# One AdaLN transformer block: the order of its first loads and scalings, and the queue of its expert rows

## What is computed

```python
mod = (_silu(c) @ wmod).reshape(8, 6, 1, 256)
sa, ca, ga, sb, cb, gb = (mod[:, i] for i in range(6))   # ga, gb: magnitude at least 0.25
h = _layernorm(x) * (1 + ca) + sa
x = x + ga * attention(h)      # W_pack to 16 q and 8 k, 8 v heads of 128; rope; 2-tap conv; window 128; W_o
h = _layernorm(x) * (1 + cb) + sb
x = x + gb * experts(h)        # h + top 4 of 32 experts (176 wide, 128 slots each) + shared expert (704 wide)
```

## Time and profile before

| | us |
|---|---|
| median of 3 runs | 781.05 |
| lowest, highest | 780.67, 781.09 |
| profiled execution, its time | 779.91 |
| its span, first to last instruction | 778.1 |
| TensorE busy in it | 744.3 (96%) |
| VectorE, ScalarE, GpSimd busy | 536.7, 441.9, 425.7 |
| DMA, mean over the span | 109 GB/s |

### The profile page before, as it was taken

The page is one execution under the profiler, slowest core; times in us unless marked ns, Lnnn a source line. Parts: engine busy times, 40 slices in busy tenths (PEclk is TensorE's granted clock), DMA queues, the critical chain, the costliest instruction groups (busy, mean ns, idle before and its releaser), DMA issues.

```text
span 778.1 us, 12285 instructions
## 1 busy us (share of the span) xinstructions
PE 744.3 (96%) x3858; PEld 617.3 (79%) x3858; DVE 536.7 (69%) x1676; ACT 441.9 (57%) x1145; POOL 425.7 (55%) x337
## 2 busy tenths in 40 slices
PE   3899999999999999999999999999989999989998
PEld 3688778888888888788888888888876777756765
DVE  4698777679877777987786798778664234534283
ACT  4687766766876576677657667766553222212110
POOL 0644445554556378646637865654544527656366
PEclk9999999999999999999999999999999999999999
DMA  8950006700005011100401101050358669997762
GB/s 301 313 130 1 2 1 207 249 1 1 1 1 174 17 39 47 39 0 1 141 23 39 46 28 45 31 161 2 122 148 265 147 189 288 271 253 149 183 203 81
DMA packets 62351, 84.45 MB, mean 109 GB/s; under 512 B 6312, under 2 KB 50229, under 8 KB 62288
## 3 DMA queue, kind: packets, MB, share of 16 engines
q1 hardware_dynamic: 52880, 73.52, 31.1%
q0 software_dynamic: 7680, 8.95, 5.8%
q10 hardware_dynamic: 1728, 1.21, 0.6%
HBM read 54.88 MB, written 33.51 MB: 114 GB/s over the span
## 4 chain that ended last, share of the span: by engine, by line
PE 78%; DVE 10%; DMA 5%; ACT 3%; issue 2%; SPq 1%; POOL 1%; ACTq 0%; POOLq 0%
PE PJ L1292 23%; PE OUT L1396 12%; PE U L1385 6%; PE U L1345 6%; PE U L1374 5%; DMA xe<-slot_rows 4%; PE U L1546 3%; PE U L1344 3%; PE U L1386 3%; PE OUT L1492 3%; PE U L1492 3%; PE U L1292 2%; PE XB L1292 2%; PE XB L1368 1%; DVE U L945 1%
## 5 line engine op out<-in xcount | busy, mean ns | idle before, releaser
L736 POOL TENSOR_TENSOR qsw<-qsw,sinT 128x512 f32<-128x512 f32 x96 | 124.2, 1294 | 214.8 <-ACT qsw L523 214.1
L536 ACT ACTIVATE U<-U,nmax 128x128 f32<-128x128 f32 (+1 forms) x256 | 98.9, 386 | 79.2 <-DVE nmax L945 79.0
L945 DVE CUSTOM_DVE_ANT_0 U<-U,mask 128x128 f32<-128x128 f32 (+1 forms) x256 | 86.6, 379 | 74.9 <-PE U L1345 74.7
L1396 PE MATMUL OUT<-wo,oT 128*128 128x256 f32 x512 | 131.5, 380 | 0.0
L1292 PE MATMUL PJ<-hT_hi,w_hi 128*128 128x512 f32 x256 | 113.5, 443 | 4.3 <-DVE hT_lo L919 3.9
L1292 PE MATMUL PJ<-hT_lo,w_hi 128*128 128x512 f32 x256 | 102.2, 399 | 0.0
L1292 PE MATMUL PJ<-hT_hi,w_lo 128*128 128x512 f32 x256 | 102.2, 399 | 0.0
L955 DVE TENSOR_SCALAR prob<-U,rinv 128x128 f32<-128x128 f32 (+1 forms) x256 | 95.1, 413 | 4.5
L522 ACT ACTIVATE qsw<-PJ 64x512 f32<-64x512 f32 x96 | 57.0, 593 | 67.1 <-PE PJ L1292 61.7
L740 POOL TENSOR_TENSOR qr<-qr,qsw 128x512 f32<-128x512 f32 x64 | 82.9, 1295 | 18.5 <-DVE qr L933 14.8
L1396 PEld LDWEIGHTS OUT<-wo,oT 128*128 128x128 f32 x512 | 87.6, 191 | 6.6
(11 more groups left out here) (201 smaller groups left out, 1557.3 us busy)
## 6 DMA issues: line engine op xcount, KB each, us to landing
wgu<-in_dram SPq DMA_DIRECT2D x32, 352.0 KB
expert_sum<-blank SPq DMA_DIRECT2D x3, 2176.0 KB, 17.7
wd<-in_dram SPq DMA_DIRECT2D x16, 352.0 KB
slot_rows<-blank SPq DMA_DIRECT2D x1, 4624.0 KB, 26.8
xe<-slot_rows SPq DMA_DIRECT2D x16, 289.0 KB
late_sums<-expert_sum SPq DMA_DIRECT2D x9, 512.0 KB, 9.8
wraw<-in_dram SPq DMA_DIRECT2D x8, 512.0 KB, 12.1
bcm<-mod_rows SPq DMA_DIRECT2D x8, 512.0 KB, 6.7
```

The costliest lines, as they stand in the source:

```text
L536: last = act.activation(U[n % 3][:, a:z], U[n % 3][:, a:z], ACT.Exp, scale=-1.0, bias=nmax[:, n % 4, j:j + 1], accum_out=rsum[:, n % 4, j: ...
L736: pool.tensor_tensor(pair3(qsw[:, n % NQSW, :]), pair3(qsw[:, n % NQSW, :]), both(sinT[:, :]), ALU.mult).then_inc(t2_done, 1)
L945: last = dve.tensor_tensor_reduce(out=U[n % 3][:, a:z], in0=U[n % 3][:, a:z], in1=mask[:, a:z], scale=-float(HD) ** -0.5, scalar=3.4e38, o ...
L1396: last = pe.matmul(OUT[b][:, t * H:(t + 1) * H], oT[:, n % NOT, t * PN:(t + 1) * PN], wo[:, head, :], start=(head == 0 and t == 0), stop=( ...
```

## The change

The first third of wmod becomes the first transfer of ScalarE's queue, ahead of the rope tables; on SyncE's queue `xin` changes places with `ident`. The second half of the first pair's features is scaled by VectorE (`prepare_second_half`) instead of ScalarE; ScalarE's two rounded copies then wait for both halves, and only one chunk of W_pack is split before the features instead of two. The first projection waits for one low part, and for the other ahead of its fourth matmul. After the transposes of `xin` TensorE does ten transposes of `ident` into the bank XB, whose result is not used. In the expert stage the rows of experts 8 to 31 are issued by ScalarE at the end of each odd slot, with the two waits that SyncE had.

```diff
+        WARM = 10
...
             sp.dma_start(c_sb[:, :], c_in).then_inc(ld_c, 16)
+            sp.dma_start(xin[:, :, :], x_pair(0)).then_inc(ld_xin, 16)
             sp.dma_start(ident[:, :], ident_t).then_inc(ld_ident, 16)
-            sp.dma_start(xin[:, :, :], x_pair(0)).then_inc(ld_xin, 16)
-            wm_src = wmod.rearrange("(c p) n -> p c n", p=PN)
-            sp.dma_start(wm[:, :, 0:2 * H], wm_src[:, :, 0:2 * H]).then_inc(ld_wm, 16)
...
             for e in range(RING, E, 2):
                 i = (e // 2) % HALF
-                sp.wait_ge(xe_ps, e + 2 - RING)
-                sp.wait_ge(told, (e - RING) // 2 + 1)
-                slot_rows(e, i)
                 sp.wait_ge(gu_ps, e + 2 - RING)
                 gate_up_weights(e, i)
...
             own = Chain(act, act_own)
+            act.dma_start(wm[:, :, 0:2 * H], wm_src[:, :, 0:2 * H]).then_inc(ld_wm, 16)
             act.dma_start(cosT[:, :], cos_t).then_inc(ld_const, 16)
...
             def prepare_hi(p, c):
-                act.wait_ge(ht_used, HC * p + (c + 1))
+                act.wait_ge(ht_used, HC * p + (c + 1) if p > 0 else HC)
...
             prepare_norm(0)
-            for n in range(W_FIRST - 1):
+            w_high(0)
+            act.wait_ge(modt_done, 1)
+            prepare_h(0, 0, U[0])
+            prepare_hi(0, 0)
+            prepare_hi(0, 1)
+            for n in range(1, W_FIRST):
                 w_high(n)
-            act.wait_ge(modt_done, 1)
-            for c in range(HC):
-                prepare_h(0, c, U[c])
-                prepare_hi(0, c)
-            w_high(W_FIRST - 1)
...
+                if n % 2 == 1 and n - 1 + RING < E:
+                    e = n - 1 + RING
+                    i = (e // 2) % HALF
+                    act.wait_ge(xe_ps, e + 2 - RING)
+                    act.wait_ge(told, (e - RING) // 2 + 1)
+                    act.dma_start(xe[:, 2 * i:2 * i + 2, :], slots_d.rearrange("(s e) h -> s e h", e=E)[:, e:e + 2, :]).then_inc(ld_xe[i], 16)
...
+            def prepare_second_half():
+                dve.wait_ge(modt_done, 1)
+                dve.wait_ge(ht_ps, 2)
+                for b in range(2):
+                    last = dve.tensor_scalar(hst[:, 1, b * S:(b + 1) * S], U[1][:, b * S:(b + 1) * S], modT[:, 3, b:b + 1],
+                                             modT[:, 1, b:b + 1], ALU.mult, ALU.add)
+                last.then_inc(ht_used, 1)
...
             mod_features()
-            for n in range(W_FIRST - 1):
-                w_low(n)
+            w_low(0)
+            prepare_second_half()
             for c in range(HC):
                 prepare_lo(0, c)
-            w_low(W_FIRST - 1)
+            for n in range(1, W_FIRST):
+                w_low(n)
...
                 for n, (c, a, b_) in enumerate(steps):
+                    if n == 3 and second is not None:
+                        pe.wait_ge(h_lo_done, second)
...
                 if l == 0:
-                    pe.wait_ge(h_lo_done, HC * (p + 1))
+                    pe.wait_ge(h_lo_done, HC * p + 1)
...
             for c in range(HC):
                 prepare_t(0, c, U[c])
+
+            for n in range(WARM):
+                pe.transpose(XB[:, 0:PN], ident[:, :], ident[:, :])
```

More of the change, by code:

```diff
@@ L290, in w_chunks @@
             return W_ORDER.index(head_of(l) * HD // WC) + 1
+        wm_src = wmod.rearrange("(c p) n -> p c n", p=PN)
         def x_pair(p):
@@ L1286, in _, with halves @@
         def _(pe):
-            def halves(out_ap, pieces, hi_lo):
+            def halves(out_ap, pieces, hi_lo, second=None):
                 (w1, w2), (x1, x2) = hi_lo
@@ L1330, in project @@
                        ((lambda c: w_hi[j][:, c, cols], lambda c: w_lo[j][:, c, cols]),
-                        (lambda c: hT_hi[:, p % 2, c, :], lambda c: hT_lo[:, p % 2, c, :]))).then_inc(pj_ps, 1)
+                        (lambda c: hT_hi[:, p % 2, c, :], lambda c: hT_lo[:, p % 2, c, :])),
+                       second=HC * (p + 1) if l == 0 else None).then_inc(pj_ps, 1)
             def scores(n):
```

## The result

The change makes the kernel faster by 0.8%: the ratio to the kernel before is 0.992, with an interval of 0.9899 to 0.9941, so 4.6 to 7.9 us of 781. The medians are 776.21 (20 runs) and 782.73; applied to the 781.05 of the prediction the ratio gives 774.8, just under the range. A second series gave 0.9904 (0.9867 to 0.9942). Ratios are of fast runs alone: a run over 1.5% above the fastest of its kernel is left out of them, though not of the medians. The forecast of 778.65, a gain of 2.4 us, had the sign and the places right and about 40% of the size; 776.21 lies near the lower end of the range.

A forecast was written before the change was run, and what follows sets the result against it. It took the start to be bound by a chain, continuous TensorE work between, and the experts by transfers. Setup -1.2 and experts -1.2 made -2.4, on the median of 781.05 giving 778.65; range 775.0 to 781.5, holding 8 in 10.

The forecast's parts named there:

- Weights first: Setup: the modulation matmuls start at 6.8, between 6.2 and 8.4, and everything behind them moves 1.6 us.
- Two engines: Setup: VectorE's scaling takes 0.86 us and ScalarE's second half leaves the line; first projection about 14.9, 3.3 us earlier.
- Identity transposes: Setup, TensorE: ten cost 2.5 us in a gap of 2.3; a faster clock in the first projection saves 0.7 of 1.55.
- The wait that takes its place: VectorE, before the second xin's statistics: stands over 3 us until that transfer lands, taken as 31.2 (31.1 to 31.6).
- The setup's term: Setup: earlier statistics of the second xin plus 0.5 us of shorter w_lo, a gain of 1.2 us (0.3 to 1.5).
- ScalarE's issues: Experts: ScalarE idles 1.90 us before the next silu, so an issue of slot rows below that costs nothing.
- The slower rival: Experts: ScalarE gets stuck in its issues of slot rows ahead of silus, losing 3.1 us; 782.95, chance 0.12.
- The experts: Expert stage: slot rows issued earlier fill idle DMA time, a gain of 1.2 us (0 to 1.8).
- the bytes stay: Expert stage: weights, rows and scatter-adds fill the DMA engines, so only idle DMA time, 1.8 us, can be gained.
- the rival in which the weights keep up: Experts: queue order, not bytes, was the limit; most of 6.1 us idling goes, 4.5 counted; 775.35, chance 0.21.
- The room at GpSimd's end: End: GpSimd's last sum ends 6.0 us before the span's end, leaving room for the 1.2, or a rival's 4.5.
- The clock in the new wait: Setup: TensorE idles during VectorE's wait, its clock halves, the next projection takes 1.55 us more; 779.85, chance 0.12.

The follow-up runs named there:

- one_engine: The changed kernel with ScalarE scaling both halves of the first pair's features, as before; ratio 0.9958 to the kernel before.
- rows_late: The kernel before with slot rows on ScalarE's queue, each load but the first issued two slots later than in the change; ratio 0.9936 to the kernel before.
- setup_only: The changed kernel with the twelve loads of slot rows back on SyncE's queue, the setup alone; ratio 0.9942 to the kernel before.
- fewer_adds: The changed kernel without the scatter-adds of the last three experts (29 to 31); ratio 0.9943 to the kernel before.
- wm_on_sp: The changed kernel with the modulation weights back on SyncE's queue, third behind ident and xin; ratio 1.0023 to the kernel before.
- rows_only: The kernel before with the twelve loads of slot rows on ScalarE's queue, that part alone; ratio 0.9932 to the kernel before.
- both: The changed kernel with the second xin ahead of the rest of wmod and GpSimd's last sum on VectorE; median 773.22, ratio 0.9917 to the kernel before.

## Why the prediction was right, and where its terms were off

*What bounds, and where.* Right: the gains sit in the first two slices and the experts, and between them nothing moves (from 38.01 to 627.29 is 589.28 us, before 40.30 to 629.45 589.15).

*Weights first.* The modulation product started at 7.52, not 6.8: its transposes waited for ident until 6.90, and ident stands behind xin now. Inside the bounds of 6.2 to 8.4.

*Two engines.* Off. VectorE's pair took 0.99 us (0.86 taken, bounds 0.69 to 1.02), but the step priced it as a gain, and one_engine shows none: both copies now wait for both halves, and VectorE's half ends 0.2 us before ScalarE would have ended it. First projection at 15.97, forecast 14.9.

*Identity transposes.* Their size was right (2.30 us against 2.5), and what they buy was taken at 0.7 of a possible 1.55; it is 1.23 at ScalarE. Their worth at the end, none, follows from the wait.

*The wait that takes its place.* Right in kind and in the row that shows it: VectorE idle before the statistics, ended by the second xin. Its size was 1.79 instead of over 3, since the landing bound was wrong: 31.1 to 31.6 was derived from the idle engine time alone, 0.33 us in one window. The statistics started at 30.31 to 30.65 in five traces, ahead of the 31 that the prediction named as a sign of being wrong. From 2 to 13 us the engines moved 314 to 324 GB/s in the traces with wm on ScalarE's queue, 288 to 298 with it on SyncE's. The 0.5 taken for w_lo became 0.73. The setup's term, 1.2 (0.3 to 1.5), is 2.2 and 1.8 at the experts' start in the two traces of after, above its bounds.

*ScalarE's issues.* The slower rival is refuted by 0.33 us each, nowhere near the 1.90 from which it decides.

*The experts.* The term was 1.2, with 1.8 as its upper end; the stage became 3.2 us shorter in the first pair of traces and 2.8 to 3.9 over the four. The failed step is "the bytes stay", from which it followed that only idle engine time could be won. That part was sized well (0.7 to 1.7 us by rows_late). Missing was that weights and rows from two queues move at a higher rate at the same busy share, and that weights are no longer issued behind rows that wait: some 2.3 us (the two are not parted). The prediction gave the rule of the Trainium skill, "DMA: Bandwidth & Descriptors", section "Issuing engines are not separate DMA queues", as one by which the term would be 0; the measurement decides against it here, 267 and 275 GB/s at the same share of 1.01. Nearest was the rival in which the weights keep up, at 775.35; it too is only half right, since four gaps with 4.07 us remain.

*The room at GpSimd's end.* Wrong. The prediction saw the last sum 6.0 us ahead of the span's end and left room for 4.5. The drain behind it took 5.3, so in that execution the room was 0.45. GpSimd's own end came only 2.00 us earlier, most of it by sums that took 23.7 us instead of 25.5, and with the 0.45 that makes the 2.43 at the program's end. That GpSimd hangs on the scatter-adds and not on TensorE was right; what was missed is that with shorter experts the chain of scatter-adds comes to hold the end, so that little of the experts' gain reaches it in this pair. In the profiled pair the two errors cancelled, and the sum of -2.4 was met by an accident of terms.

*The clock in the new wait.* This rival had 0.12 and asked for a fall from full clock, which no row shown of before has. It exists. In the windows of setup_only the first has TensorE idling for half its time, the second the clock; the third is the first window in after:

```profile
30.00:34.00 4.00, 2.05 (x10) 1.43 (x9) 2.88 (x12) 2.46 (x8) 2.39 (x2) 0.99 1.11 277
34.00:37.40 3.40, 3.40 (x12) 2.92 (x11) 3.16 (x10) 2.19 (x8) 2.10 (x3) 0.50 1.08 238
```

```profile
30.00:34.00 4.00, 1.71 (x10) 1.17 (x9) 3.09 (x13) 2.15 (x7) 2.54 (x2) 1.00 1.11 263
```

It fell there, to 1.2 GHz, in three of ten traces of kernels with this setup or most of it (also in fewer_adds and wm_on_sp), not in the two of after. The first W_o product then starts at 39.06 and 38.84 instead of 38.01 to 38.35: 0.5 to 1 us, not the 1.55 that the rival named. The idling alone doesn't decide it: in after TensorE idles longer in that window, and no fall follows. What does is not shown.

*How fine the measurement is.* The prediction took 0.2%, 1.6 us, as what can be told from no change. The interval of the main series is 0.4% wide, those of the variants some 0.7%.

*What stays open.* The terms that the traces show, some 2 us of setup and 1 to 3 behind the experts, make 3 to 5 us; the ratio says 4.6 to 7.9. Each kernel has only one traced execution or two, and two of the same kernel before differ by 2.0 us in the chain of scatter-adds alone (87.9 and 89.9 us from first to last). The mean granted clock, which is on record for nearly every run, narrows it. One slope for all kernels, fitted over the 240 runs that the ratios use and whose clock is on record, gives 6.2 us (0.7 either way) for each 0.01 that the granted clock, as a share of full speed, is lower, and leaves 2 us from run to run. By this fit, an estimate that is good to about 1 us, the times at a clock of 0.995 are:

| kernel | before, on three chips | after | setup_only | rows_only | rows_late | wm_on_sp | both |
|---|---|---|---|---|---|---|---|
| us | 782.0, 782.5, 783.6 | 775.9, 776.2 | 781.0 | 777.7 | 778.6 | 778.7 | 774.3 |

So the clock isn't what parts the two kernels: the change is worth some 7 us at equal clock. On the chip of setup_only and rows_only (before: 783.6) the setup gives some 2.5 and the rows 5.9. The setup's part is that of the traces; of the rows' 5.9 the stage of the experts shows 3 to 4, and where the rest lies was not settled. The term that was mis-sized most is the experts'.

## What to carry to other kernels

Before giving a step room behind a stage, read each engine's last instruction to the program's end, closing drains included, and not its last busy row. Where one queue carries both transfers that wait for something and transfers that others wait for, ask what a second queue does to the rate itself, not only to the idle time. When a stage gets shorter, follow the chain of the new profile: another engine's work that used to fit under it may now hold the end. Of a setup chain shortened in three places, only the part that moved the next late transfer was kept: find that transfer first. Where executions of one kernel differ by more than the change is worth, compare them at equal clock before reading a single trace's end.

## What the runs showed of the hardware

With the expert rows moved from SyncE's to ScalarE's queue, issued no earlier, the DMA engines moved 275 instead of 267 GB/s at the same busy share of 1.01; over 68 us of the stage, GB/s divided by the share are 272 to 276 in the eleven traces with that move (ten of them with the early issue) and 263 to 267 in the three without. GpSimd's closing drain ended 5.3 us behind its last sum in before, in after and with one sum less. VectorE's sum of 128x1024 took 1.22 us alone and up to 3.4 us beside GpSimd's sums. TensorE's clock fell to half for 3.4 us near 250 us in ten of fourteen traces, while TensorE was busy throughout the stretch, and in before over the 12.7 us ahead of it as well. Before's row is:

```profile
252.70:256.10 3.40, 3.40 (x10) 2.71 (x10) 0.77 (x3) 0.83 (x2) 0.00 (x0) 0.50 0.33 115
```
